# The causal mask of the diagonal score blocks: from a GpSimd multiply after the softmax numerator to an identity matmul into PSUM before it

## The chip, the cores and the metric

One core of one Trainium2 chip. The metric is the device time of one execution in microseconds. Engines are named as the profile names them: PE is TensorE (PEld its weight loads), DVE is VectorE, ACT is ScalarE, POOL is GpSimd, SP is SyncE, which only issues DMAs here.

## The reference

Two residual blocks over x of shape (2, 2048, 512) in float32. The first is causal attention with 16 heads of 32 features over a conditional linear layer, the second an adapter, a layer norm and an int8 linear layer. The change touches the attention:

```python
scores = jnp.einsum('bhtd,bhsd->bhts', q, k) * scale
alibi = -jnp.abs(rel).astype(jnp.float32) * alibi_slopes[None, :, None, None]
scores = scores + alibi
scores = jnp.where(causal[None, None], NEG, scores)      # causal = key after query
num = 0.5 * (1.0 + scores * jax.lax.rsqrt(1.0 + scores * scores))
probs = num / (jnp.sum(num, axis=-1, keepdims=True) + eps)
out = jnp.einsum('bhts,bhsd->bhtd', probs, v)
```

The softmax is a rational one: no maximum, no exponential. A masked score of -10000 has a numerator of about zero.

## The kernel before

The work is cut into 8 groups: 2 batches times 4 groups of 4 heads (`HG`). Within a group the 2048 queries are 4 chunks of 512 (c = 0 to 3), and chunk c meets the key blocks kb = 0 to 4c+3 of 128 keys each. One chunk and one key block are a unit (40 in a group); a unit has two pairs of heads, k = 2u and 2u+1, so a group has 80 pairs and the kernel 640. In scores keys lie on the partitions and queries along the free axis, two heads side by side.

The last four key blocks of every chunk lie on the diagonal (`g.diag`, 16 units and 32 pairs of a group, 256 pairs in all). There the queries before the key block are left out, so the widths of a pair are 1024, 768, 512 and 256 elements, two pairs of each in a chunk, and of what is left the first 128 queries of each head form the triangle that has to be masked. I call the 8 pairs on the diagonal of one chunk a diagonal stretch, and the pairs ahead of them, all 1024 wide, a full stretch (0, 8, 16 and 24 pairs for c = 0 to 3). There are 32 diagonal stretches.

For each pair, in this order:

1. PE writes two score matmuls into one of two PSUM slots `sc` (L835). It waits until DVE has read the pair two before (`s_g`).
2. ACT squares the scores into `yb` (L677), then takes 1/sqrt(1 + square) in place (L679). The `yb` ring has 4 places, so L677 waits for the numerator of the pair four before (`s_num`).
3. DVE forms g = score * y into `gb` (L1049). This frees the PSUM slot.
4. POOL squares y in place (L626); ACT takes (1 + g) squared in place, two pairs late (L669).
5. DVE adds the two, two pairs late (`NUM_LAG`, L990): y*y + (1+g)*(1+g) = 2(1+g), the numerator.
6. On diagonal pairs POOL multiplies the triangle's 128 queries of both heads by a 0/1 matrix `causal` (L605), after its own square of the pair two later (`MASK_LAG`).
7. PE multiplies the numerators of a whole unit with the values into `ov` and with ones into `dn` (L815), three units late (`LAG`). It waits for `s_mask` on diagonal units and for `s_num` on the others. At a chunk's first unit it waits for DVE to have copied the previous chunk out of `ov` and `dn` (L1003 and L1004, in the form for the previous group L1085 and L1086).

The order on every engine is written out by hand in `Group.events`; between the pairs lie parts of other jobs (projections of the next chunks at L731 and L735, the conditional layer at L748, and in some groups the adapter and the layer norm). Every engine works strictly along its list. The two middle head groups of each batch, 4 of the 8 groups, carry only the projections; I call them plain groups. The first group of batch 0 also makes the rest of that batch's conditional layer (opening), the last of batch 0 that of batch 1 (closing), the first of batch 1 the adapter work of batch 0 (joined), and the last one that of batch 1 (ending).

Of the kernel before, what the change touches and what calls it, by code (L numbers as in the profile page):

```python
# [7 lines left out]
ALU = mybir.AluOpType  # L8
# [8 lines left out]
P = 128  # L17
# [11 lines left out]
MASK_LAG = 2  # L29
# [3 lines left out]
MAGIC = 12582912.0  # L33
SOFT_EPS = 4e-6
# [129 lines left out]
def adaln_attn_ffn(nc, x, ids_cond, ids_lang, cond_w, cond_b, w_qkv, w_out, slopes, W1, b1, W2, b2,  # L164
# [34 lines left out]
    UNITS, PAIRS, DIAG = len(plain.units), 2 * len(plain.units), len(plain.diag)  # L199
# [39 lines left out]
    with ExitStack() as ctx:  # L239
# [21 lines left out]
        causal = sb("causal", [P, P])  # L261
# [53 lines left out]
        s_mask = sem("s_mask")  # L315
# [268 lines left out]
        def _(pool):  # L584
# [7 lines left out]
            pool.memset(causal[:, :], 1.0).then_inc(s_const, 1)  # L592
            pool.wait_ge(s_const, 6)
            pool.affine_select(out=causal[:, :], in_=causal[:, :], compare_op=ALU.is_ge, fill=0.0, base=0,
                               pattern=[[1, P]], channel_multiplier=-1).then_inc(s_const, 1)
            pool.memset(qmv[0:32, :, :, :].bitcast(F32), 0.0).then_inc(s_zero, 1)
            pool.wait_ge(s_al, 32)
            pool.memset(kst[0:32, :, :].bitcast(F32), 0.0).then_inc(s_zero, 1)

            def mask(G, g, k):  # L600

                q0 = q0_of(g, k)
                pool.wait_ge(s_num, G * PAIRS + k + 1)
                t = gview(k)[:, :, q0:q0 + P]
                pool.tensor_tensor(t, t, causal[:, :].unsqueeze(1).to_broadcast([P, 2, P]), ALU.mult).then_inc(s_mask, 1)  # L605
# [16 lines left out]
            def group(b, hg, G, g, base):  # L622
                def scored(k):
                    y = yview(k)[:, :, q0_of(g, k):]
                    pool.wait_ge(s_g, G * PAIRS + k + 1)
                    pool.tensor_tensor(y, y, y, ALU.mult).then_inc(s_y2, 1)  # L626
                    m = k - MASK_LAG
                    if (m >= 0 or g is not opening) and m // 2 % UNITS in g.diag:
                        mask(G, g, m)


                k = None
                for e in g.events:
                    if e[0] in ("qk", "pv") and k is not None:
                        scored(k)
                        k = None
                    if e[0] == "qk":
                        k = e[1]
                    elif e[0] == "step":
                        after(b if g is ending else b - 1, e[1], base)  # L640

            for_groups(pool, group)
            for m in range(-MASK_LAG, 0):
                mask(B * NG, plain, m)
# [59 lines left out]
        def _(pe):  # L704
# [98 lines left out]
            def products(G, g, u):  # L803

                c, kb = g.units[u % UNITS]
                q0 = g.width(u % UNITS)
                if u % UNITS in g.diag:
                    pe.wait_ge(s_mask, 2 * (G * DIAG + g.diag.index(u % UNITS) + 1 - (DIAG if u < 0 else 0)))
                else:
                    pe.wait_ge(s_num, G * PAIRS + 2 * u + 2)  # L810
                last_kb = kb == TT * (c + 1) - 1
                for dst, is_v in ((ov, True), (dn, False)):
                    for h in range(HG):
                        lhsT = vv[:, kb, h * D:(h + 1) * D] if is_v else ones[:, :]
                        r = pe.matmul(dst[h * D:(h + 1) * D, q0:], lhsT, gview(2 * u + h // 2)[:, h % 2, q0:],  # L815
                                      start=(kb == 0), stop=last_kb)
                r.then_inc(s_pv, 1)

            def group(b, hg, G, g, base):
                item, carry = 0, g is not opening  # L820
                for e in g.events:
                    if e[0] == "qk":
# [10 lines left out]
                        for i in range(2):  # L833
                            h = 2 * (k % 2) + i
                            r = pe.matmul(slot[:, i, q0:], kst[:, h, kb * P:(kb + 1) * P],  # L835
                                          qmv[:, c % 2, h, q0:], start=True, stop=True)
# [23 lines left out]

            for_groups(pe, group)
# [286 lines left out]
```

## Time and profile before

| | |
|---|---|
| median of 3 runs | 2297.26 us (2292.51 to 2299.26) |
| profiled execution, span from first to last instruction | 2294.5 us |
| PE busy | 1763.6 us (77%) |
| DVE busy | 1917.8 us (84%) |
| ACT busy | 1686.5 us (74%) |
| POOL busy | 1901.6 us (83%) |
| POOL mask multiplies (L605) | 256 instructions, 248.2 us |
| granted TensorE clock, mean | 0.903 |

Busy is the time in which the engine has an instruction running. No time is recorded for what surrounds the span of the profiled execution; the span is 2.8 us under the median of the runs. A granted clock of 1.00 is TensorE's full 2.4 GHz; it has one lower level, 1.2 GHz, and a figure between 0.5 and 1 is a mixture over the stretch. The pairs run from about 89 us to 2165 us of the span; what lies before is the preparation of the weights, what lies behind the end of the layer norm work and the int8 matmul.

### The profile page before, as it was taken

How to read it: one execution, taken by the hardware profiler on the slowest of the kernel's cores; microseconds unless marked ns; L12 is line 12 of the kernel's file. 1: busy time of each engine (PE TensorE's matmuls, PEld its weight loads, DVE VectorE, ACT ScalarE, POOL GpSimd, SP SyncE). 2: the span in 40 equal slices, each digit the busy share in tenths (PEclk: the TensorE clock that was granted, in tenths of full speed). 3: DMA queues.
4: the chain of work that ended last, by engine and by line, in shares of the span. 5: the costliest groups of instructions: out<-in, count | busy, mean ns of one | idle time of the engine just before them, and what ended most of it. 6: DMA issues, size and time to landing. Idle time of an engine off the chain costs nothing.

```text
span 2294.5 us, 30517 instructions
## 1 busy us (share of the span) xinstructions
PE 1763.6 (77%) x10128; PEld 873.0 (38%) x10128; DVE 1917.8 (84%) x2114; ACT 1686.5 (74%) x1938; POOL 1901.6 (83%) x1038
## 2 busy tenths in 40 slices
PE   5678877777787788998888876777687777786864
PEld 4555332323332345664444333333332333342331
DVE  4358888888889899898898898888889898899758
ACT  0247897889789888888656567889889888767413
POOL 2147998999989998898888888999989998898648
PEclk9899988888888899999999998888889898898879
DMA  5411111111111022202222221111111031121137
GB/s 177 140 48 43 48 34 30 47 40 30 34 39 48 20 80 60 69 18 81 76 75 80 65 57 30 43 44 27 38 39 48 20 85 39 39 65 47 51 123 239
DMA packets 126618, 138.64 MB, mean 60 GB/s; under 512 B 27868, under 2 KB 78044, under 8 KB 126044
## 3 DMA queue, kind: packets, MB, share of 16 engines
q1 hardware_dynamic: 126460, 136.64, 21.1%
q8 instruction: 86, 1.41, 0.3%
q14 instruction: 72, 0.59, 0.1%
HBM read 54.02 MB, written 22.80 MB: 33 GB/s over the span
## 4 chain that ended last, share of the span: by engine, by line
PE 24%; POOL 24%; DVE 19%; issue 14%; ACT 13%; SPq 2%; DMA 2%; DVEq 0%; POOLq 0%; ACTq 0%
POOL yb L626 18%; DVE gb L990 6%; ACT yb L677 6%; DVE gb L1049 5%; ACT yb L679 5%; PE sc L835 4%; PE ov L815 4%; PE it L748 3%; PE dn L815 3%; ACT gb L669 3%; PE it L731 3%; PE it L755 3%; POOL gb L605 2%; PE it L735 2%; POOL oT L662 2%
## 5 line engine op out<-in xcount | busy, mean ns | idle before, releaser
L626 POOL TENSOR_TENSOR yb<-yb 128x1024 f32<-128x1024 f32 (+3 forms) x640 | 1468.5, 2301 | 310.2 <-DVE gb L1049 296.0
L677 ACT ACTIVATE yb<-sc 128x1024 f32<-128x1024 f32 (+3 forms) x640 | 567.1, 886 | 398.8 <-PE sc L835 310.6
L990 DVE TENSOR_TENSOR gb<-gb,yb 128x1024 f32<-128x1024 f32 (+3 forms) x640 | 817.2, 1277 | 36.7 <-POOL yb L626 35.3
L1049 DVE TENSOR_TENSOR gb<-sc,yb 128x1024 f32<-128x1024 f32 (+3 forms) x640 | 676.4, 1057 | 150.3 <-ACT yb L679 147.2
L835 PE MATMUL sc<-qmv,kst 128*128 128x512 f32 (+3 forms) x1280 | 473.7, 458 | 333.7 <-DVE gb L1049 317.4
L679 ACT ACTIVATE yb<-yb 128x1024 f32<-128x1024 f32 (+3 forms) x640 | 595.1, 930 | 20.3
L669 ACT ACTIVATE gb<-gb 128x1024 f32<-128x1024 f32 (+3 forms) x640 | 584.1, 913 | 0.8 <-DVE gb L1049 0.8
L835 PEld LDWEIGHTS sc<-qmv,kst 128*128 128x128 f32 x1280 | 216.3, 206 | 699.8 <-DVE gb L1049 520.0
L815 PE MATMUL ov<-gb,vv 128*32 128x512 f32 (+3 forms) x2560 | 337.8, 603 | 37.2 <-DVE den L1086 15.3
L815 PE MATMUL dn<-gb,ones 128*32 128x512 f32 (+3 forms) x2560 | 326.4, 584 | 0.0
L731 PE MATMUL it<-hT,wT 128*128 128x512 f32 x496 | 254.6, 639 | 5.8 <-DVE area L928 1.8
L605 POOL TENSOR_TENSOR gb<-gb,causal 128x256 f32<-128x256 f32 x256 | 248.2, 970 | 0.0
L815 PEld LDWEIGHTS dn<-gb,ones 128*32 128x32 f32 x2560 | 89.4, 120 | 181.7 <-issue 176.2
L748 PE MATMUL it<-area 128*128 128x128 f32 x1024 | 131.3, 284 | 23.2 <-DVE area L911 21.8
L748 PEld LDWEIGHTS it<-area 128*128 128x128 f32 x1024 | 127.2, 199 | 31.7 <-DVE area L911 26.7
L731 PEld LDWEIGHTS it<-hT,wT 128*128 128x128 f32 x496 | 100.8, 205 | 87.2 <-issue 68.3
L735 PE MATMUL it<-wT,hT 128*128 128x128 f32 x992 | 128.0, 284 | 4.2 <-DVE stage L908 3.5
L735 PEld LDWEIGHTS it<-wT,hT 128*128 128x128 f32 x992 | 126.9, 200 | 11.4 <-DVE stage L908 3.8
L755 PE MATMUL it<-area,oT 128*128 128x512 f32 x224 | 116.2, 647 | 19.3 <-DVE area L918 6.4
L815 PEld LDWEIGHTS ov<-gb,vv 128*32 128x32 f32 x2560 | 52.8, 113 | 168.2 <-issue 115.8
L715 PE MATMUL it<-ident,area 128*128 128x128 f32 x336 | 53.0, 291 | 33.5 <-DMA area<-in_x_dram 13.0
L1014 DVE TENSOR_TENSOR oT<-oT,den 128x512 f32 (+1 forms) x31 | 65.9, 2124 | 1.9 <-DMA den<-rec_d 1.9
(109 smaller groups left out, 1020.4 us busy)
## 6 DMA issues: line engine op xcount, KB each, us to landing
qmv<-stage SPq DMA_DIRECT2D x384, 64.0 KB
kst<-stage SPq DMA_DIRECT2D x384, 64.0 KB
area<-in_x_dram SPq DMA_DIRECT2D x58, 256.0 KB, 2.8
out_dram<-oT SPq DMA_DIRECT2D x32, 256.0 KB, 3.5
den<-rec_d SPq DMA_DIRECT2D x31, 256.0 KB
wT<-wT_d SPq DMA_DIRECT2D x7, 768.0 KB, 4.4
x_d<-area SPq DMA_DIRECT2D x16, 256.0 KB, 2.6
z_d<-area SPq DMA_DIRECT2D x16, 256.0 KB, 3.1
```

What stands on the lines that cost most here:

```text
L605: pool.tensor_tensor(t, t, causal[:, :].unsqueeze(1).to_broadcast([P, 2, P]), ALU.mult).then_inc(s_mask, 1)
L626: pool.tensor_tensor(y, y, y, ALU.mult).then_inc(s_y2, 1)
L669: act.activation(t, t, ACT.Square, bias=1.0).then_inc(s_g2, 1)
L677: act.activation(y, sc[:, k % SLOTS, :, q0_of(g, k):], ACT.Square).then_inc(s_s2, 1)
L679: act.activation(y, y, ACT.Abs_reciprocal_sqrt, bias=1.0).then_inc(s_y, 1)
L731: r = pe.matmul(bank, wT[:, "qk".index(what), part, :], hT[:, part, c * CH:(c + 1) * CH], **ends)
L735: r = pe.matmul(bank[:, part * P:(part + 1) * P], hT[:, k, tok], wT[:, 2, k, :], start=(k == 0), stop=(k == KC - 1))
L748: r = pe.matmul(bank[:, part * P:(part + 1) * P], wc[:, k, part * P:(part + 1) * P], xT[:, a, k, :], start=(k == 0), stop=(k == KC - 1))
L815: r = pe.matmul(dst[h * D:(h + 1) * D, q0:], lhsT, gview(2 * u + h // 2)[:, h % 2, q0:], start=(kb == 0), stop=last_kb)
L835: r = pe.matmul(slot[:, i, q0:], kst[:, h, kb * P:(kb + 1) * P], qmv[:, c % 2, h, q0:], start=True, stop=True)
L990: dve.tensor_tensor(t, t, yview(k)[:, :, q0:], ALU.add).then_inc(s_num, 1)
L1049: dve.tensor_tensor(gview(k)[:, :, q0:], sc[:, k % SLOTS, :, q0:], yview(k)[:, :, q0:], ALU.mult).then_inc(s_g, 1)
```

## The change

The mask is no longer multiplied onto the weights. A constant 128x128 matrix `unseen`, -1e12 where the key lies after the query and 0 elsewhere, is made once, as is a bf16 copy of it and of the identity. Behind each score matmul of a diagonal pair PE issues one more matmul, identity times `unseen16`, 128 columns in bf16, which accumulates onto the first 128 queries of that head's scores in PSUM. At -1e12 the two squares that follow add to nearly zero. POOL's `mask` and its semaphore are gone, and the products wait for `s_num` in every unit.

```diff
-MASK_LAG = 2
+UNSEEN = -1e12
...
-            pool.memset(causal[:, :], 1.0).then_inc(s_const, 1)
+            pool.memset(unseen[:, :], 0.0).then_inc(s_const, 1)
             pool.wait_ge(s_const, 6)
-            pool.affine_select(out=causal[:, :], in_=causal[:, :], compare_op=ALU.is_ge, fill=0.0, base=0,
+            pool.affine_select(out=unseen[:, :], in_=unseen[:, :], compare_op=ALU.is_ge, fill=UNSEEN, base=0,
                                pattern=[[1, P]], channel_multiplier=-1).then_inc(s_const, 1)
+            pool.wait_ge(s_const, 7)
+            pool.tensor_copy(unseen16[:, :], unseen[:, :]).then_inc(s_const, 1)
+            pool.tensor_copy(ident16[:, :], ident[:, :]).then_inc(s_const, 1)
...
-            def mask(G, g, k):
-
-                q0 = q0_of(g, k)
-                pool.wait_ge(s_num, G * PAIRS + k + 1)
-                t = gview(k)[:, :, q0:q0 + P]
-                pool.tensor_tensor(t, t, causal[:, :].unsqueeze(1).to_broadcast([P, 2, P]), ALU.mult).then_inc(s_mask, 1)
...
                     pool.tensor_tensor(y, y, y, ALU.mult).then_inc(s_y2, 1)
-                    m = k - MASK_LAG
-                    if (m >= 0 or g is not opening) and m // 2 % UNITS in g.diag:
-                        mask(G, g, m)
...
-                if u % UNITS in g.diag:
-                    pe.wait_ge(s_mask, 2 * (G * DIAG + g.diag.index(u % UNITS) + 1 - (DIAG if u < 0 else 0)))
-                else:
-                    pe.wait_ge(s_num, G * PAIRS + 2 * u + 2)
+                pe.wait_ge(s_num, G * PAIRS + 2 * u + 2)
...
+                            on_diagonal = k // 2 in g.diag
                             r = pe.matmul(slot[:, i, q0:], kst[:, h, kb * P:(kb + 1) * P],
-                                          qmv[:, c % 2, h, q0:], start=True, stop=True)
+                                          qmv[:, c % 2, h, q0:], start=True, stop=not on_diagonal)
+                            if on_diagonal:
+                                r = pe.matmul(slot[:, i, q0:q0 + P], ident16[:, :], unseen16[:, :], start=False, stop=True)
...
+            pe.wait_ge(s_const, 9)
             for_groups(pe, group)
```

What stands on PE in the last two units of a chunk's diagonal, before (ov and dn are the products with the values and with ones, sc the scores):

```order
L835 MATMUL sc<-qmv,kst 128x256 [waits s_g]
L835 MATMUL sc<-qmv,kst 128x256
L815 MATMUL ov<-gb,vv 32x512 [waits s_num]
L815 MATMUL ov<-gb,vv 32x512 x3
L815 MATMUL dn<-gb,ones 32x512 x4
```

and after the change, at the same place, for the pair ahead of the same products:

```order
L825 MATMUL sc<-qmv,kst 128x256 [waits s_g]
L828 MATMUL sc<-unseen,ident 128x128
L825 MATMUL sc<-qmv,kst 128x256
L828 MATMUL sc<-unseen,ident 128x128
L804 MATMUL ov<-gb,vv 32x512 [waits s_num]
```

Each pair has two more matmuls, each with a weight load of its own, between and behind the score matmuls; nothing else on PE has changed its place. On POOL a diagonal stretch reads, before:

```order
L626 TENSOR_TENSOR yb<-yb 128x2x384 [waits s_g]
L605 TENSOR_TENSOR gb<-gb,causal 128x2x128 [waits s_num]
L625 REGISTER_ALU
L626 TENSOR_TENSOR yb<-yb 128x2x256 [waits s_g]
L605 TENSOR_TENSOR gb<-gb,causal 128x2x128 [waits s_num]
```

and after:

```order
L623 TENSOR_TENSOR yb<-yb 128x2x384 [waits s_g]
L622 REGISTER_ALU
L623 TENSOR_TENSOR yb<-yb 128x2x256 [waits s_g]
L622 REGISTER_ALU
L623 TENSOR_TENSOR yb<-yb 128x2x256 [waits s_g]
```

POOL's list is the squares alone, and it no longer waits for anything that DVE does after g. The lists of ACT, DVE and SP are the same as before.

## Rows read from the trace of the kernel before

**Rows 1.** The page, part 1: busy, share of the span, instructions

```profile
PE 1763.6 (77%) x10128; PEld 873.0 (38%) x10128; DVE 1917.8 (84%) x2114; ACT 1686.5 (74%) x1938; POOL 1901.6 (83%) x1038
```

**Rows 2.** Busy by stretch: diagonal stretches of the plain groups, sum of 16

```profile
core 0: us, PE busy (x) PEld busy (x) DVE busy (x) ACT busy (x) POOL busy (x), PEclk, DMA share, GB/s
...
493.79:514.92 21.13, 14.93 (x92) 4.91 (x82) 17.62 (x17) 17.15 (x25) 20.84 (x14) 0.84 0.00 1
...
sum 345.12, PE 253.41 PEld 94.21 DVE 279.60 ACT 273.04 POOL 329.86; mean PE 15.84 PEld 5.89 DVE 17.47 ACT 17.06 POOL 20.62
```

**Rows 3.** Busy by stretch: full stretches of the plain groups, sum of 12

```profile
sum 595.12, PE 456.48 PEld 207.11 DVE 533.99 ACT 549.02 POOL 529.96; mean PE 38.04 PEld 17.26 DVE 44.50 ACT 45.75 POOL 44.16
```

**Rows 4.** Busy by stretch: diagonal stretches of the other groups, sum of 16

```profile
94.13:143.37 49.24, 33.67 (x209) 26.66 (x210) 20.73 (x28) 15.87 (x23) 18.24 (x14) 0.90 0.19 49
...
893.24:915.12 21.88, 20.22 (x166) 13.61 (x164) 19.51 (x23) 17.13 (x26) 21.88 (x15) 1.00 0.21 57
...
1257.27:1290.15 32.88, 27.80 (x136) 12.33 (x134) 29.06 (x47) 15.44 (x23) 30.55 (x22) 0.90 0.20 55
...
sum 400.31, PE 314.38 PEld 162.03 DVE 327.65 ACT 263.57 POOL 347.14; mean PE 19.65 PEld 10.13 DVE 20.48 ACT 16.47 POOL 21.70
```

**Rows 5.** Timeline, 500 to 517: start, us, instruction, idle before it

```profile
508.95 1.94 PE L815 MATMUL ov<-gb,vv 128*32 128x512 f32 x8
...
509.25 0.38 ACT L677 ACTIVATE yb<-sc 128x256 f32<-128x256 f32 x1 [1.56 <-DVE gb L990]
...
510.00 0.73 POOL L605 TENSOR_TENSOR gb<-gb,causal 128x256 f32<-128x256 f32 x1
510.08 1.20 DVE L990 TENSOR_TENSOR gb<-gb,yb 128x512 f32<-128x512 f32 x1 [0.60 <-POOL yb L626]
...
512.77 1.02 ACT L677 ACTIVATE yb<-sc 128x1024 f32<-128x1024 f32 x1 [2.17 <-PE sc L835]
...
516.23 2.00 POOL L626 TENSOR_TENSOR yb<-yb 128x1024 f32<-128x1024 f32 x1 [0.38 <-DVE gb L1049]
```

**Rows 6.** Groups by line and shape: xcount, busy us, mean ns, idle before

```profile
L605 POOL TENSOR_TENSOR gb<-gb,causal 128x256 f32<-128x256 f32 x256 | 248.2, 970 | 0.0
...
L990 DVE TENSOR_TENSOR gb<-gb,yb 128x512 f32<-128x512 f32 x64 | 67.6, 1056 | 23.9 <-POOL yb L626 23.9
...
L1049 DVE TENSOR_TENSOR gb<-sc,yb 128x512 f32<-128x512 f32 x64 | 43.3, 676 | 1.6 <-ACT yb L679 1.6
```

**Rows 7.** Timeline, a full stretch: nine squares in a row; a numerator

```profile
541.01 26.40 POOL L626 TENSOR_TENSOR yb<-yb 128x1024 f32<-128x1024 f32 x9 [1.67 <-DVE gb L1049]
...
543.79 1.22 DVE L990 TENSOR_TENSOR gb<-gb,yb 128x1024 f32<-128x1024 f32 x1
```

**Rows 8.** Timeline and groups: runs of 128-column matmuls on PE

```profile
99.36 6.41 PE L748 MATMUL it<-area 128*128 128x128 f32 x56
```

**Rows 9.** One line, L880 and L748: ns min/median/max, bf16 and f32

```profile
L880 PEld LDWEIGHTS sc<-wT,yb x128: 95/98/147, 2232.0 to 2281.8; 128*128 128x128 bf16 x128
...
L748 PEld LDWEIGHTS it<-area x1024: 186/192/338, 18.1 to 1033.5; 128*128 128x128 f32 x171
L748 PE MATMUL it<-area x1024: 270/275/553, 18.2 to 1033.6; 128*128 128x128 f32 x171
```

**Rows 10.** Waits: who for whom, us in total, times, longest

```profile
ACT yb L677 <- PE sc L835: 310.6, 166, 19.0
...
PEld ov L815 <- POOL gb L605: 21.5, 23, 3.5
...
PE ov L815 <- POOL gb L605: 10.7, 13, 2.6
```

**Rows 11.** Timeline, 384 to 401, the turn from chunk 0 to chunk 1

```profile
391.00 1.94 PE L815 MATMUL ov<-gb,vv 128*32 128x512 f32 x8 [2.78 <-DVE den L1086]
...
394.57 1.55 PE L835 MATMUL sc<-qmv,kst 128*128 128x512 f32 x4
...
395.69 1.02 ACT L677 ACTIVATE yb<-sc 128x1024 f32<-128x1024 f32 x1 [4.56 <-PE sc L835]
```

More of the change, by code:

```diff
@@ L198, in adaln_attn_ffn @@
                         after_jobs(j, first[j // TT + 1] + 2 * LAG + 2 * NORM_LAG + 3, first[NC] - 9 + j - KB + TT, first[NC] - 1)], False, slack=0.3)
-    UNITS, PAIRS, DIAG = len(plain.units), 2 * len(plain.units), len(plain.diag)
+    UNITS, PAIRS = len(plain.units), 2 * len(plain.units)
     assert PAIRS % YRING == 0 and PAIRS % GRING == 0
@@ L260, in adaln_attn_ffn @@
         ones = sb("ones", [P, D])
-        causal = sb("causal", [P, P])
+        unseen = sb("unseen", [P, P])
+        unseen16 = sb("unseen16", [P, P], BF16)
+        ident16 = sb("ident16", [P, P], BF16)
         cbias = sb("cbias", [P, KC])
@@ L314, in adaln_attn_ffn @@
         s_num = sem("s_num")
-        s_mask = sem("s_mask")
         s_pv = sem("s_pv")
@@ L642, in _ @@
             for_groups(pool, group)
-            for m in range(-MASK_LAG, 0):
-                mask(B * NG, plain, m)
             for job in END_JOBS:
```

## The prediction

> **What bounds the kernel now.** I read the page first. Four engines are busy for 74 to 84% of the span [rows 1], so no engine bounds the whole kernel, and the share of POOL that the mask takes (248 us [rows 6]) says nothing yet. The question is which engine is full in the stretches where the mask is. So I cut the span where DVE starts the g of the first pair of each full and each diagonal stretch, and read the busy time of every engine in each piece.
>
> In the plain groups the 12 full stretches (192 pairs) last 595.1 us, 3.10 us a pair; ACT is busy for 549.0 of it, 92%, DVE and POOL for 534 and 530 [rows 3]. In the 16 diagonal stretches (128 pairs) it is otherwise: 345.1 us, 21.6 a stretch, of which POOL is busy for 329.9, 96%, DVE for 279.6, ACT for 273.0 and PE for 253.4 [rows 2]. There POOL is the bound, and by a wide margin: 20.6 us a stretch against 17.5, 17.1 and 15.8. In the other groups' 16 diagonal stretches POOL is first too, with 347.1 of 400.3 us, but DVE has 327.7 and PE 314.4 [rows 4].
>
> The timeline shows how POOL's lateness reaches the rest: DVE's numerator stands idle for 0.60 us until POOL's square is there, and ACT's next square waits 1.56 us for a numerator, because the ring `yb` is full [rows 5]. The mask also reaches DVE directly. The numerator that starts at 510.08 beside a mask takes 1.20 us; over all its 64 instances that shape takes 1.056 us, while g, of the same width but with one input in PSUM, takes 0.676 [rows 5, 6].
>
> **The change, part by part.**
>
> *The mask leaves POOL.* 256 instructions of 0.970 us, 248 us of POOL time [rows 6]. In a plain diagonal stretch that is up to 8 x 0.970 = 7.8 us (6 of its own in most windows, as two masks run into the next stretch), so POOL falls from 20.6 us to some 13 to 15. DVE gets back what the overlap cost: 1.056 - 0.676 = 0.38 us on a numerator at 512 wide is the most that it can be; at 0.3 us for 8 numerators it falls from 17.5 to about 15. ACT's 17.1 us does not move. With PE as it is, ACT would be next, at 17.1.
>
> *Two matmuls a pair are added to PE.* No row of before has this bf16 matmul. A run of 56 f32 matmuls of 128 columns, each with its weight load, takes 6.41 us, 0.114 us for load and matmul together at the full clock [rows 8]. A bf16 weight load takes 98 ns where the f32 one takes 192 [rows 9], so 0.114 is a ceiling for throughput at the full clock. The floor is nothing, if the two fit where PE idles. I take 0.114: 16 matmuls in a stretch are 1.8 us at full clock. The quoted stretch has a granted clock of 0.84 [rows 2], and if the added work fell wholly on the 1.2 GHz level it would be 3.7 us. PE then has 15.8 + 1.8 = 17.6 us, up to 19.5 us, and is the fullest engine, ahead of ACT. [...]
>
> *What a plain diagonal stretch then takes.* POOL at 20.6 us busy gave 21.6 us, 96%. PE is interrupted more often, since it takes turns with ACT and DVE through two PSUM slots; with PE at 17.6 us and 94% I get 18.8 us. That is 2.8 us less than 21.6, times 16: **-45 us**. Bounds: ACT's busy time alone, 17.1 us a stretch, gives -72; PE at 19.5 us and 93% gives 21.0 and -10.
>
> *The other groups' diagonal stretches.* The first, 49.2 us, has POOL busy for only 18.2 [rows 4], so it gains nothing. In the other fifteen, 351 us, POOL has 328.9 us and DVE 306.9. DVE has more other work here, as in the stretch of 32.9 us with DVE at 29.1 and POOL at 30.6, and in the closing group PE has 20.2 of 21.9 us at full clock [rows 4]; 1.8 us more there fills the stretch by itself. What DVE can get back is 15 x 8 x 0.3 = 36 us, the most that this part can gain is thus about 45, and the least about 5. I take 1.7 us a stretch: **-26 us**.
>
> *The masks that run over.* After each of 24 diagonal stretches that is followed by a full one, two masks run at the start of the full stretch, against 1024 wide squares and numerators. ACT bounds those stretches, so most is hidden; I take 0.4 us each: **-10 us**, between 0 and -20.
>
> *The added time lies on the way from score to ACT.* At the turn of a chunk ACT waits for PE already: 2.17 us at 512.77, behind 1.94 us of products at half clock [rows 5], and 4.56 us at 395.69, where PE first waited 2.78 us for DVE to empty `dn`, then needed 3.6 us for products (391.00 to 394.57) before the next score [rows 11]. Three more matmul pairs pass ahead of such a score in the same time. I take 0.5 us for each of the 24 turns: **+12 us**, between 0 and 25. Within a stretch PE has the score of a pair ready ahead of ACT, except in the 256 wide pairs, and I add nothing.
>
> *The wait of the products.* On diagonal units PE waited for the mask 10.7 us (13 times) and its weight loads 21.5 us [rows 10]. The products of unit u stand behind the scores of pair 2u+7, which wait for g of pair 2u+5; on DVE the numerator of pair 2u+1 precedes that g. So `s_num` is always there in time, and this wait ends. It is inside the terms above. Nothing new is queued behind it. The two POOL copies at the start and PE's wait for `s_const` cost nothing: the pairs begin near 89 us and the constants are made at the head of POOL's list, ahead of a long idle time.
>
> Sum: -45 - 26 - 10 + 12 = -69 us against the profiled execution's 2294.5 us: 2225.5. The median of the runs is 2.8 us above that span, so I predict **2228 us**.
>
> **The shared port, as a check.** Nine squares of 1024 take 26.40 us, 2.93 each, beside DVE's numerator of 1.22 [rows 7]; one with DVE idle takes 2.00 [rows 5]. So POOL and DVE cost each other about 0.8 us a pair. The Trainium skill (SBUF — State Buffer, Who interferes with whom) says that a VectorE instruction with two SBUF inputs and a GpSimd instruction take turns on one port, the later one blocked entirely. By that rule a pair of a full stretch would need 2.00 + 1.22 = 3.22 us on the port; the trace has 2.93, so they overlap in part. The rule would put the mask's price at its own 0.73 us plus the same again on DVE, and the gain nearer to that of the second case below.
>
> **The rivals.**
>
> *Larger gain, 2165 us, chance 0.18.* PE's matmuls fit into its idle time and bring a higher granted clock (0.84 in the quoted stretch), and DVE gets everything back. Then ACT is the bound: -72 - 45 - 15 = -132 from 2297. For it: PE is idle for a quarter of these stretches. Against it: at the turns ACT already waits for PE with POOL's lateness not in the chain.
>
> *Nearly nothing, 2282 us, chance 0.12 (half of it within 0.3% of before).* POOL's lateness only hid that of DVE and PE: -10 - 5 and +12 at the turns, and a few us of run-over masks, give -8 to -20. For it: DVE has 17.5 and 29.1 us in stretches of 21 and 33. This is also the case in which the change removes work and no wait.
>
> *Slower, 2360 us, chance 0.08.* The two matmuls lie in the ring PE, ACT, DVE, PE over two PSUM slots. A single 128-column matmul takes 0.275 us from start to end [rows 9], and if each of the two adds that whole, a pair is 0.55 us later, 256 x 0.55 = +141 us. Against that stand the -81 us of the first three terms: +60, 2357 or about 2360. It decides from 81/256 = 0.32 us a pair on the path. Against it: such matmuls follow each other every 0.114 us, and PE idles before most scores.
>
> **How the numbers follow.** My forecast has 0.62, with 2195 to 2262 as its own range. Faster by over 0.3% (about what a measurement of this kernel can tell from none): 0.62 + 0.18 + 0.06 = 0.86; within 0.3%: 0.06; slower: 0.08. The range reaches from inside the larger gain to inside the small one, 2175 to 2275, which leaves out under 2 in 10.
>
> **What would show it.** POOL's busy time down by some 248 us, to 1650; the 512 wide numerator down from 1.056 to near 0.7 us; the diagonal stretches of the plain groups at 18 to 19.5 us with PE the fullest engine, full stretches within 1 us of before; each added matmul spaced by 0.06 to 0.12 us. I am wrong if those stretches stay above 20.5 us, or if PE's wait for g shrinks while ACT's wait for scores (310.6 us now [rows 10]) grows by more than it.

## The result and the profile after

The changed kernel takes 2266.89 us (median of 4 runs, 2263.74 to 2269.1) against 2297.82 us for the kernel before on the same chip. The ratio is 0.9875, with a 95% interval of 0.9863 to 0.9888. That is a gain of 31 us by the medians, 26 to 31 us by the interval. It is faster, as forecast, and inside the range of 2175 to 2275, but the forecast gain was 69 us: less than half of it came. The profiled execution's span is 2263.8 us, against 2294.5.

The page of the kernel after, parts 1 and 4 (busy time of each engine; then the chain that ended last, by engine):

```profile
PE 1803.9 (80%) x10640; PEld 904.5 (40%) x10640; DVE 1878.6 (83%) x2114; ACT 1685.0 (74%) x1938; POOL 1715.7 (76%) x784
...
PE 38%; ACT 21%; DVE 20%; issue 12%; POOL 4%; DMA 2%; SPq 2%; DVEq 0%; POOLq 0%; ACTq 0%
```

POOL lost 186 us of busy time [rows 1], where 248 us of masks were taken away, and POOL has all but left the chain, where it had 24% before; PE went from 24% to 38%. The squares (L626, now L623) had 18% of the chain before; they have 16 us of it now, under 1%, and most of the 4% left is outside the attention. Of the missing 62 us, 42 went into longer squares (busy for 1468.5 us before and 1510.2 now), and 18 were never there to be freed, since the records of the masks overlapped those of POOL's other work. The groups by line and shape, beside [rows 6] (columns as there):

```profile
L623 POOL TENSOR_TENSOR yb<-yb 128x1024 f32<-128x1024 f32 x448 | 1189.2, 2663 | 394.1 <-DVE gb L1042 382.2
...
L983 DVE TENSOR_TENSOR gb<-gb,yb 128x1024 f32<-128x1024 f32 x448 | 613.3, 1369 | 1.7
...
L623 POOL TENSOR_TENSOR yb<-yb 128x768 f32<-128x768 f32 x64 | 155.8, 2448 | 38.0 <-DVE gb L1042 37.9
L828 PE MATMUL sc<-unseen,ident 128*128 128x128 bf16 x512 | 121.8, 243 | 0.0
L623 POOL TENSOR_TENSOR yb<-yb 128x512 f32<-128x512 f32 x64 | 108.9, 1713 | 15.1 <-DVE gb L1042 15.1
...
L983 DVE TENSOR_TENSOR gb<-gb,yb 128x512 f32<-128x512 f32 x64 | 56.0, 875 | 1.5 <-ACT gb L661 0.5 <-POOL yb L623 0.3
...
L828 PEld LDWEIGHTS sc<-unseen,ident 128*128 128x128 bf16 x512 | 52.6, 103 | 47.8 <-issue 27.6
```

The squares got longer. At 512 wide they took 1537 ns before and take 1713 now, at 768 wide 2247 and now 2448. That they run beside DVE's numerators more of the time is my reading; run 12 below shows that the squares slow the numerators. DVE's numerator at 512 wide fell from 1056 to 875 ns only, not to the 700 that I had named; over all 640 numerators the mean went from 1277 to 1218 ns, 38 us, where I had counted on up to 77.

The diagonal stretches of the plain groups, cut as in [rows 2]:

```profile
374.05:396.86 22.81, 16.81 (x114) 7.57 (x113) 15.72 (x21) 16.09 (x25) 14.50 (x8) 0.78 0.15 37
...
490.06:510.84 20.78, 16.07 (x104) 6.25 (x96) 16.78 (x17) 17.37 (x25) 16.36 (x9) 0.84 0.01 2
...
sum 339.12, PE 273.12 PEld 113.92 DVE 265.05 ACT 269.94 POOL 261.63; mean PE 17.07 PEld 7.12 DVE 16.57 ACT 16.87 POOL 16.35
```

PE's 17.1 us and ACT's 16.9 are what the forecast said (17.6 and 17.1), and POOL is down to 16.4. But the stretch takes 21.2 us, not 18.8: no engine is busy for more than 81% of it, where POOL had 96% of the time before. The full stretches of the plain groups, cut as in [rows 3]:

```profile
sum 589.52, PE 459.71 PEld 207.30 DVE 526.02 ACT 551.39 POOL 504.24; mean PE 38.31 PEld 17.27 DVE 43.84 ACT 45.95 POOL 42.02
```

All 640 pairs, cut in the same way (us; the sum of each kind, and what lies behind the last g):

| | before | after | difference | forecast |
|---|---|---|---|---|
| plain groups, 16 diagonal stretches | 345.1 | 339.1 | -6.0 | -45 |
| other groups, 16 diagonal stretches | 400.3 | 394.5 | -5.8 | -26 |
| all 24 full stretches | 1325.3 | 1312.4 | -12.9 | -10 |
| turns of a chunk (inside the rows above) | | | | +12 |
| behind the last g | 129.6 | 124.0 | -5.6 | 0 |

Every difference of stretches here and below comes from one profiled execution of each kernel. By chunk, the plain diagonal stretches changed by +0.8, -5.6, -1.1 and -0.2 us (c = 0 to 3, four stretches each): nearly all of the gain is in chunk 1. The plain full stretches changed by -5.1 us at chunk 1, +0.6 at chunk 2 and -1.1 at chunk 3.

The last row is a term that I left out. Behind the last g the last masks and the products that wait for them ended 7.2 us later in the kernel before and end 2.4 us later now, and the rest of the program follows them.

Why the diagonal stretches hardly moved is seen in what each engine waited for there. Idle time before an instruction, by what ended it, summed over the 16 plain diagonal stretches (us, waits of more than 0.15 us alone; "no mask" is run 1 below, without POOL's mask and without the matmuls):

| who waits, for what | before | no mask | after |
|---|---|---|---|
| DVE's numerator, for POOL's square | 19.6 | none | 0.3 |
| ACT's square, for a numerator (the ring `yb` is full) | 22.2 | 6.8 | 7.1 |
| ACT's square, for a score of PE | 43.8 | 48.0 | 57.8 |
| DVE's g, for ACT | 23.3 | 23.3 | 31.3 |
| PE's score, for g | 73.4 | 64.8 | 54.1 |

The two waits that POOL caused are gone or down to a third. But ACT was idle for 66.0 us in these stretches before and is for 64.9 now: it waits for scores instead of numerators. Twice as much of its idle time was for scores as for numerators even in the kernel before. The chain says the same. In the stretch that [rows 2] shows, POOL was busy for 20.84 of 21.13 us, and it has no piece of the chain there (before, 493.79 to 514.92, by line; the view cuts the line off):

```profile
by line: issue 24.0%; DVE gb L1049 13.9%; ACT yb L677 12.6%; ACT yb L679 11.8%; ACT gb L669 9.9%; PE ov L815 8.8%; PE sc L835 6.4%; PE dn L815 5.6%; DVE oT L1014 3.7%; DVE gb L990 2.9%; DVEq L1048 0.4%; DVEq L1011 0.2%; DVEq L1012 0.2%; DVE
```

Over the 16 plain diagonal stretches before, POOL has 62 of the chain's 345 us, in five of the stretches, and PE has 100. After, POOL has none and PE 155.

The chain from 493 to 508, in order of time (start, us, what), shows what stands in a diagonal stretch now:

```profile
493.01 1.24 DVE gb L1042
494.25 0.04 issue
494.29 0.69 PE sc L825
494.98 0.13 PE sc L828
495.11 0.43 PE sc L825
495.54 0.13 PE sc L828
495.67 1.87 PE ov L804 x8
497.53 1.71 PE dn L804 x8
499.24 0.51 PE sc L825
...
502.74 1.47 issue
504.21 0.09 DVE oT L1007
...
504.81 0.69 DVE gb L1042
...
505.54 0.33 PE sc L825
505.87 0.07 PE sc L828
505.94 0.12 PE sc L825
506.06 0.07 PE sc L828
506.13 1.00 PE ov L804 x8
507.13 0.86 PE dn L804 x8
```

Two kinds of work stand ahead of a score: 3.6 us of products at the 1.2 GHz level (granted clock 0.50 from 494.25 to 500.4; the same products take 1.9 us from 506.13, at 1.00), and on DVE a numerator and a division of the previous chunk (L1007) ahead of the g that frees the PSUM slot. Neither has a term of its own in my sum, except products at the turns. The experiments ask whether they are the reason.

### The profile page after: what moved, and what is told of

Read it like the earlier page. It is cut to its first block, busy times and chain, and to the rows that moved or that the text cites. A ratio compares the mean times of both kernels' runs of the same rounds, so it can differ in the third digit from the quotient of the medians.

```text
span 2263.8 us, 31228 instructions
## 1 busy us (share of the span) xinstructions
PE 1803.9 (80%) x10640; PEld 904.5 (40%) x10640; DVE 1878.6 (83%) x2114; ACT 1685.0 (74%) x1938; POOL 1715.7 (76%) x784
## 4 chain that ended last, share of the span: by engine, by line
PE 38%; ACT 21%; DVE 20%; issue 12%; POOL 4%; DMA 2%; SPq 2%; DVEq 0%; POOLq 0%; ACTq 0%
ACT yb L669 9%; PE sc L825 7%; PE ov L804 7%; ACT yb L671 7%; DVE gb L1042 6%; PE dn L804 6%; ACT gb L661 6%; DVE gb L983 5%; PE it L723 5%; PE it L740 4%; PE it L747 4%; PE it L727 3%; POOL oT L654 2%; SPq L428 2%; PE it L707 1%
## 5 line engine op out<-in xcount | busy, mean ns | idle before, releaser
L623 POOL TENSOR_TENSOR yb<-yb 128x1024 f32<-128x1024 f32 (+3 forms) x640 | 1510.2, 2373 | 460.9 <-DVE gb L1042 448.6
L983 DVE TENSOR_TENSOR gb<-gb,yb 128x1024 f32<-128x1024 f32 (+3 forms) x640 | 779.2, 1218 | 3.9 <-ACT gb L661 0.5
L825 PE MATMUL sc<-qmv,kst 128*128 128x512 f32 (+3 forms) x1280 | 505.6, 472 | 295.8 <-DVE gb L1042 278.2
L825 PEld LDWEIGHTS sc<-qmv,kst 128*128 128x128 f32 x1280 | 238.7, 209 | 648.3 <-DVE gb L1042 453.3
L804 PE MATMUL ov<-gb,vv 128*32 128x512 f32 (+3 forms) x2560 | 338.4, 604 | 18.0 <-DVE den L997 10.5
L723 PE MATMUL it<-hT,wT 128*128 128x512 f32 x496 | 249.9, 629 | 5.8 <-DVE area L921 1.8
L727 PEld LDWEIGHTS it<-wT,hT 128*128 128x128 f32 x992 | 121.1, 194 | 8.8 <-DVE stage L901 2.5
L828 PE MATMUL sc<-unseen,ident 128*128 128x128 bf16 x512 | 121.8, 243 | 0.0
L804 PEld LDWEIGHTS ov<-gb,vv 128*32 128x32 f32 x2560 | 52.4, 112 | 133.4 <-issue 82.2
L899 DVE TENSOR_SCALAR stage<-it 128x512 fp32r<-128x512 f32 x64 | 43.7, 683 | 34.7 <-PE it L723 20.8
```

The costliest lines, as they stand in the source:

```text
L723: r = pe.matmul(bank, wT[:, "qk".index(what), part, :], hT[:, part, c * CH:(c + 1) * CH], **ends)
L727: r = pe.matmul(bank[:, part * P:(part + 1) * P], hT[:, k, tok], wT[:, 2, k, :], start=(k == 0), stop=(k == KC - 1))
L983: dve.tensor_tensor(t, t, yview(k)[:, :, q0:], ALU.add).then_inc(s_num, 1)
```

## The experiments

Every ratio is to the kernel before, measured on the same chip in turns (its medians: 2296.09 us beside runs 1 to 4, 2292.79 beside 5 to 8, 2295.05 beside 9 to 11, 2296.70 beside 12 and 13). "Plain" is the sum of the plain groups' 16 diagonal stretches, "diagonal" that of all 32. The expectations of runs 1 to 4 are by two theories: A, that POOL's lateness lay beside other waits that are nearly as long, so that its mask is worth little and the matmuls cost little; B, that the POOL mask is worth the forecast 81 us and the matmuls take some 50 of them back.

**1 to 4. The two prices apart.** No mask at all (the output then lacks it):

```diff
                             r = pe.matmul(slot[:, i, q0:], kst[:, h, kb * P:(kb + 1) * P],
-                                          qmv[:, c % 2, h, q0:], start=True, stop=not on_diagonal)
-                            if on_diagonal:
-                                r = pe.matmul(slot[:, i, q0:q0 + P], ident16[:, :], unseen16[:, :], start=False, stop=True)
+                                          qmv[:, c % 2, h, q0:], start=True, stop=True)
```

> The changed kernel without the added matmuls: the causal mask is left out altogether, so keys after the query count in the diagonal blocks. Theory A (POOL's lateness lay beside a wait of PE, ACT and DVE on each other that is nearly as long, and the added matmuls cost little): 2255 to 2265 us, at most 12 us under the changed kernel's 2266.9. Theory B (taking the mask off POOL is worth the forecast 81 us, and the added matmuls take some 50 of them back): about 2220 us, under 2235 in any case.

Both masks, POOL's multiplies and PE's matmuls:

```diff
+                    if (m >= 0 or g is not opening) and m // 2 % UNITS in g.diag:
+                        mask(G, g, m)
...
+                if u % UNITS in g.diag:
+                    pe.wait_ge(s_mask, 2 * (G * DIAG + g.diag.index(u % UNITS) + 1 - (DIAG if u < 0 else 0)))
```

> The changed kernel with POOL's multiply put back as well, so both masks are applied: POOL is as loaded as before and PE as loaded as after. Theory A: 2296 to 2305 us, within 8 us of the kernel before, since PE's added time lies under POOL's lateness. Theory B: the added matmuls cost some 50 us here too, 2330 us or more, unless POOL's lateness hides them. Together with the run without any mask this gives the price of each of the two, with and without the other.

The mask matmul issued twice for each head:

```diff
+                                r = pe.matmul(slot[:, i, q0:q0 + P], ident16[:, :], unseen16[:, :], start=False, stop=False)
                                 r = pe.matmul(slot[:, i, q0:q0 + P], ident16[:, :], unseen16[:, :], start=False, stop=True)
```

> The changed kernel with every mask matmul issued twice (the constant is added two times). Theory A: 5 to 10 us over the changed kernel, 2272 to 2277. Theory B: as much again as the first matmuls took, 2300 us or more.

Both score matmuls of a pair first, then both mask matmuls:

```diff
-                            if on_diagonal:
-                                r = pe.matmul(slot[:, i, q0:q0 + P], ident16[:, :], unseen16[:, :], start=False, stop=True)
+                        if on_diagonal:
+                            for i in range(2):
+                                r = pe.matmul(slot[:, i, q0:q0 + P], ident16[:, :], unseen16[:, :], start=False, stop=True)
```

> The changed kernel with both score matmuls of a pair first and the two mask matmuls behind them, so that the second score matmul's weights load under the first one as before the change. In the trace of the changed kernel a pair's scores are complete about 0.20 us later than before at full clock. Theory A: 0 to 3 us faster than the changed kernel, 2264 to 2267. Theory B: a third or more of the price of the matmuls comes back, 2250 us or less.

| | POOL mask | mask matmuls | us | ratio (95%) | plain | diagonal |
|---|---|---|---|---|---|---|
| before | yes | 0 | 2296.09 | 1 | 345.1 | 745.4 |
| 2, both | yes | 2 a pair | 2310.59 | 1.0063 (1.0037 to 1.0089) | 353.3 | 751.8 |
| after | no | 2 a pair | 2266.89 | 0.9875 (0.9863 to 0.9888) | 339.1 | 733.6 |
| 3, twice | no | 4 a pair | 2275.37 | 0.9905 (0.9881 to 0.9929) | 345.6 | 742.5 |
| 4, masks last | no | 2 a pair | 2260.36 | 0.9841 (0.9818 to 0.9864) | 335.5 | 731.9 |
| 1, no mask | no | 0 | 2256.19 | 0.9817 (0.9788 to 0.9846) | 330.2 | 720.7 |

The matmuls cost 13.3 us without the POOL mask (0.9875 less 0.9817, of 2296) and 14.5 us with it; two more a pair cost 7 us. With the intervals these are 6 to 21, 8 to 20 and 1 to 13 us. Taking the mask off POOL is worth 42 us without the matmuls (40 by the medians) and 43 with them, so the two prices add up. Runs 1 and 3 lie in A's ranges, and B failed in all four. A failed in run 2, where it had at most 8 us over the kernel before: the matmuls cost as much in stretches in which POOL is busy for 94% of the time as in those where it is not, so a full POOL does not hide them. Run 4 is faster than A's range and slower than B's. The surprise is run 1: with no mask anywhere, the kernel gains only 40 us. My forecast has ACT as the bound in that case, at 17.1 us a stretch; it is 330.2 / 16 = 20.6, with ACT busy for 82% of it:

```profile
sum 330.21, PE 253.45 PEld 92.24 DVE 269.42 ACT 270.25 POOL 265.99; mean PE 15.84 PEld 5.77 DVE 16.84 ACT 16.89 POOL 16.62
```

Masks last is the best version that computes all of it: 7.8 us below the change as made by the ratios. It is not certain: the two intervals touch (0.9864 and 0.9863), and its profiled execution has a span of 2264.9 us, beside 2263.8.

**5 to 8. Products ahead of a score, and the division (theories P and D).** First the products were split, those with the values ahead of the odd pair's scores, those with ones behind them:

```diff
+                        if k % 2 and early(g, k // 2 - LAG):
+                            products(G, g, k // 2 - LAG, (0,))
...
-                        products(G, g, u)
+                        products(G, g, u, (1,) if early(g, u) else (0, 1))
```

> The changed kernel with the products of a unit in two parts: the four matmuls into ov are issued ahead of the odd pair's scores, the four into dn stay behind them (a chunk's first unit stays whole). Work, buffers and the DVE list are the same. Theory P (what took POOL's place is PE: a block of 2.0 us of products, 3.6 at half clock, stands between an odd and an even pair's scores, and ACT runs dry behind it): 8 to 20 us faster than the changed kernel, 2247 to 2259. Theory D (it is DVE's list: the division, the copies and the numerators that stand ahead of g): no change, 2264 to 2270.

Then chunk 1's division was moved to a later pair, into the full stretch:

```diff
-                lag = NORM_LAG_LAST if c == NC - 1 else NORM_LAG
+                lag = NORM_LAG_LAST if c == NC - 1 else 3 if c == 1 else NORM_LAG
```

> The changed kernel with the division of chunk 1 (one 2 us instruction of DVE in each of the 8 groups) moved from the narrow pairs of chunk 2's diagonal, at pair 45, to pair 38 of its full stretch. Theory D: g of pair 45 no longer stands behind it, 1 to 2 us a group, 8 to 16 us faster, 2251 to 2259. Theory P: 0 to 4 us faster, since PE's products are next at the same place.

Then the products with ones were left out, except at the first and the last key block of a chunk, in the kernel after and in the one before (the denominators are then too small):

```diff
-                for dst, is_v in ((ov, True), (dn, False)):
+                for dst, is_v in ((ov, True), (dn, False))[:2 if kb == 0 or last_kb else 1]:
```

> The changed kernel without most of the denominators' products: the four matmuls into dn are issued for the first and the last key block of a chunk alone, so the denominators are too small. PE loses some 250 us of its work and the block ahead of the next scores is halved. Theory P: the diagonal stretches of the plain groups fall to 18.5 us or less and the whole to 2220 us or less. Theory D: 2250 us or more.

> The kernel before with the same products left out. Theory P: POOL is the bound with or without PE's products, so it stays within 20 us of the kernel before, 2277 to 2297, and its distance to the changed kernel with the same omission is 60 us or more, near the 81 that was forecast for the relief of POOL. Theory D: the distance stays at 30 to 40 us.

| | us | ratio (95%) | plain | diagonal |
|---|---|---|---|---|
| 5, split | 2274.61 | 0.9917 (0.9895 to 0.9938) | 338.4 | 736.3 |
| 6, division moved | 2278.34 | 0.9931 (0.9913 to 0.9949) | 332.1 | 723.9 |
| 7, after, few products | 2238.66 | 0.9746 (0.9721 to 0.9771) | 332.5 | 719.8 |
| 8, before, few products | 2277.10 | 0.9925 (0.9905 to 0.9945) | 339.0 | 741.0 |

Both rearrangements are slower than the change as made (0.9875), by 10 and 13 us, and neither theory had that: P expected run 5 to be faster and D run 6, and none expected a slower kernel. The moved division did shorten the plain diagonal stretches by 7.0 us, but the plain full stretches grew from 589.5 to 601.0: it costs more there, where ACT is busy for 94% of the time. Run 7 is also between the theories: its plain diagonal stretches take 20.8 us each and not 18.5, but its time is under D's 2250. With half of the products gone the change is worth 38 us instead of 31, as D had it, not the 60 and more of theory P. Leaving the products out gives 30 us in the kernel after (0.9875 to 0.9746) and 17 in the one before: PE is nearer to the bound after the change, but these products account for 7 of the 38 us that lie between the 69 forecast and the 31 measured.

**9. The granted clock (theory K).** Ten bf16 matmuls of zeros were added behind the even diagonal pairs of chunks 1 to 3:

```diff
+                        if c and k % 2 == 0 and k // 2 in g.diag:
+                            for _ in range(10):
+                                pe.matmul(dn[:, 0:P], zero16[:, :], ident16[:, :], start=False, stop=False)
```

> The changed kernel with ten bf16 matmuls of a zero matrix, 128 columns each, accumulated onto dn behind the scores of every even diagonal pair of chunks 1 to 3: they add nothing to the result and keep TensorE at work where it idles 1.6 to 2.1 us for DVE's g. Theory K (the lower clock, 0.75 to 0.92 in these stretches of the plain groups, is what makes the products behind it long, 3.6 us where full clock takes 2.0): the granted clock of these stretches rises to 0.95 or more and the time falls by 10 to 20 us, to 2247 to 2257. Theory T (PE, ACT and DVE wait for each other in turn and each is nearly as long as POOL was): the clock may rise, but the ten matmuls stand ahead of the next scores and DVE is next anyway: 2262 to 2275.

2281.35 us, ratio 0.9949 (0.993 to 0.9967), 17 us slower than the change as made, and outside both theories' ranges. The granted clock of those twelve plain stretches went from between 0.84 and 1.00 to 1.00 in ten of them, and to 0.95 and 0.91 in the other two. All 16 plain stretches together take 339.4 us, where they took 339.1, but that hides three different things (us, four stretches each):

| | chunk 0, no zeros | chunk 1 | chunk 2 | chunk 3 |
|---|---|---|---|---|
| after | 93.0 | 77.6 | 84.7 | 83.9 |
| with zeros | 94.9 | 77.8 | 80.3 | 86.5 |

At chunk 2 the clock of all four rose from between 0.84 and 0.87 to 1.00, and each is 0.7 to 1.5 us shorter, as K would have it, 4.4 us in all; in the other chunks the sums did not fall. In the closing group, where PE is full, the full stretches grew by 4.3 us and the diagonal ones by 4.6. So the zeros cost more than the clock gave back.

**10 and 11. Products and division both relieved.** Few products with ones, and the division cut to one column (the output of the attention is then not divided):

```diff
-                dve.tensor_tensor(o, o, den[:, :], ALU.mult).then_inc(s_norm, 1)
+                dve.tensor_tensor(o[:, 0:1], o[:, 0:1], den[:, 0:1], ALU.mult).then_inc(s_norm, 1)
```

> The changed kernel without most of the denominators' products, as in the last pair of experiments, and with each 2 us division of DVE in the loop cut to one column, so that the output is not normalised: PE loses some 250 us of work and DVE some 60. Theory T: with PE and DVE both relieved nothing stands in POOL's place but ACT: 2205 us or less. Theory C (the mask off POOL is worth 40 us whatever the others do, since its time on the shared port returns as longer squares and numerators): 2225 us or more.

> The kernel before with the same two omissions. Theory T: POOL still bounds its diagonal stretches, 2260 to 2275 us, and the distance to the changed kernel with the same omissions is 55 us or more. Theory C: the distance stays at 35 to 45 us.

2234.28 us, ratio 0.9740 (0.9723 to 0.9758) for the kernel after, and 2252.71 us, 0.9822 (0.9801 to 0.9842) for the one before. Run 10 by itself is as C had it, but run 11 is below T's range, and the difference of the two is 18 us, under what either theory gave, so both failed. The finding is by ratios beside runs 7 and 8: the cut division gives 24 us while POOL has its masks, and 1 to 4 us without them. The plain diagonal stretches did not move (334.3 and 339.9). In the kernel before POOL is busy for 326.5 of the 339.9 us; after the change no engine is above 82%. All versions with the squares in them stay at 20.6 us a stretch or more.

**12 and 13. The squares and the mask.** One thing that all these versions share is POOL's squares beside DVE's numerators. Here the diagonal pairs' squares are taken on 16 queries of each head only (the rest of y*y is left out), in the kernel after and in the one before:

```diff
+                    if k // 2 in g.diag:
+                        y = y[:, :, 0:16]
                     pool.tensor_tensor(y, y, y, ALU.mult).then_inc(s_y2, 1)
```

> Leaves most of the diagonal pairs' y*y out: on POOL only the first 16 queries of each head are squared, so in a diagonal stretch POOL works some 2 us instead of 12, and takes no time from DVE. The mask is in the PE matmuls as in the kernel after. Theory S (what is left of the plain diagonal stretches, 21.2 us each, hangs on POOL and DVE sharing time: squares of up to 2.66 us and numerators of 1.37): the plain diagonal stretches fall from 339.1 to below 315 us in sum, all 32 from 733.6 to below 695, and the time from 2267 to 2225 to 2235. Theory R (it hangs on the ring PE, ACT, DVE over two PSUM slots, in which POOL's square has no part, and on ACT and DVE work that stays): the plain diagonal stretches stay above 330, and the time is 2255 to 2267.

> The kernel before with the same cut: POOL's squares on diagonal pairs on 16 queries of each head only, so POOL's share there is its mask multiplies (7.8 us a stretch) and little else. If POOL's total length is what the mask costs in the kernel before, the mask is now hidden, and moving it to PE is worth nothing or loses: this kernel is at most 3 us slower than the kernel after with the same cut, or up to 14 us faster (what the two matmuls a pair cost in the runs with and without them). If the mask's place in the order (numerator, then mask, then products) or its sharing of time with DVE costs by itself, this kernel is 10 us or more slower than it.

| | squares whole | squares cut | the cut is worth |
|---|---|---|---|
| mask on POOL: us (ratio) | 2297 (1) | 2235.29 (0.9727) | 61 us |
| mask on PE: us (ratio) | 2267 (0.9875) | 2246.01 (0.9780) | 21 us |
| moving the mask is worth | -31 us | +10.7 us | |
| diagonal, mask on POOL | 745.4 | 693.0 | 52.4 |
| diagonal, mask on PE | 733.6 | 715.1 | 18.5 |

The differences are those of the medians; by the ratios the cut is worth 63 and 22 us. The intervals are 0.9707 to 0.9747 and 0.9764 to 0.9797. Once POOL has room, the change of this document makes the kernel 10.7 us slower: 22.1 us more in the diagonal stretches, 9.5 less in the full ones (1322.2 to 1312.7), where the masks that run over no longer stand, and 1.6 less behind the last g. The plain groups' diagonal stretches, cut as in [rows 2], mask on PE first:

```profile
418.60:438.11 19.51, 17.24 (x124) 7.24 (x123) 15.73 (x20) 16.65 (x25) 8.52 (x9) 0.91 0.19 51
...
sum 332.01, PE 271.09 PEld 113.35 DVE 245.64 ACT 268.99 POOL 122.16; mean PE 16.94 PEld 7.08 DVE 15.35 ACT 16.81 POOL 7.63
```

and mask on POOL:

```profile
419.45:437.50 18.05, 14.53 (x110) 5.79 (x108) 16.16 (x20) 16.48 (x25) 13.50 (x15) 1.00 0.21 56
...
sum 313.28, PE 235.09 PEld 89.11 DVE 252.84 ACT 269.14 POOL 204.54; mean PE 14.69 PEld 5.57 DVE 15.80 ACT 16.82 POOL 12.78
```

With the mask on POOL they are 19.6 us each, the first of all versions under 20.5; with the mask on PE 20.8, where PE is busy for 16.9 us a stretch instead of 14.7. With the mask on PE, DVE's numerators fell from 1292 to 991 ns at 768 wide and from 875 to 708 at 512 as the squares beside them were cut; with the mask on POOL those at 512 fell from 1056 to 976. For run 12 neither theory was right: the stretches stayed above 330 us as R says, the time came out between the two, as did the sum over all 32. For run 13 the first branch was right: with POOL's time short enough, its mask is hidden.

## Why the prediction fell short

**"There POOL is the bound, and by a wide margin": half right.** POOL was the fullest engine, and its lateness cost time: leaving out its squares gives 61 us, 52 of them in the diagonal stretches. But it was not the bound alone and not by a wide margin. Leaving out its masks gives 40 us, the added matmuls lengthened the plain diagonal stretches by 8.2 us while POOL was full (345.1 to 353.3, run 2), and ACT was idle for scores twice as long as for anything that POOL held up. I read the margin from busy times, 20.6 against 17.5, and a busy time says nothing of how long the waits of the others are.

**"What a plain diagonal stretch then takes", 18.8 us: the step that failed.** I took the fullest engine's busy time, PE's 17.6, and divided it by 94%. The busy time was right (17.1), the 94% was not: it was 81%. A share of 96% was what one overfull engine reached. With four engines at 16.4 to 17.1 us, each of which takes turns with the others, the stretch has no such engine. The matmuls on PE are not the reason: without them (run 1) the share is 82% and the stretch 20.6 us. What the runs show in place of my step is that the waits changed hands. Without the POOL mask and with nothing added, ACT's idle time in these stretches fell by 11.2 us in sum (66.0 to 54.8), DVE's for squares by 19.6, and the stretches by 14.9, where my step would have given 54 (ACT's 17.1 us by 94% is 18.2 a stretch); with the matmuls ACT's idle time is back at 64.9. Which wait between PE, ACT and DVE holds the stretch at 20.6 us is not shown: relieving PE (run 7), PE and DVE (run 10) and the clock (run 9) each left the mean above 20.5, and only cutting POOL's squares with the mask on POOL (run 13) brought it lower.

**The turns, +12 us: wrong.** The turn that I quoted shows nothing: ACT waits 4.62 us for the score at 394.71, where it waited 4.56 before [rows 11]. Over all 24 turns ACT's idle time before the first pair's square fell, from 64.7 to 58.0 us, and it is 60.1 without the matmuls (run 1). The matmuls' price is real, 13 us, but it lies within the diagonal stretches (733.6 against 720.7), where I had counted the matmuls as busy time of PE and added nothing for them on the way from score to ACT.

**The other groups, -26 us: DVE's relief was mis-sized**, and the term measured -5.8. DVE's busy time there fell by 9.6 us (327.7 to 318.1), where I had up to 36, and PE's grew by 22.5 (314.4 to 336.9); one stretch of the opening group grew from 23.9 to 26.3 us. What DVE gets back was sized at 0.3 us for each numerator. It is 0.18 at 512 wide and 0.17 at 256 (592 to 427 ns), nothing at 768 (1263 to 1292), 0.04 at 1024. My reading is that the squares, which now stand closer to the numerators, took it; no run shows that by itself. The row behind my check by the shared port was misread a little: the square of 2.00 us at 516.23 had no numerator beside it for most of its time, but DVE was not idle, its g ran from 517.23. By that check each mask would have cost DVE another 0.73 us; DVE's busy time fell by 39 us for all 256, 0.15 each.

**The masks that run over: right in sum** (-12.9 against -10), by luck in its parts. I had 0.4 us at each of 24 stretches. The plain groups' full stretches of chunk 1 went from 26.0 to 26.3 down to 24.9 us each, and those of chunks 2 and 3 by 0.5 in sum over eight. **The drain behind the last g, -5.6 us, was left out.**

**The added matmul: right.** In the chain above it has 0.13 us at the 1.2 GHz level, and 0.07 at the full clock (505.87); I had said 0.06 to 0.12. A load takes 96 ns by the median where the f32 one takes 192; that is a factor of two, as in [rows 9]. The Trainium skill (TensorE: Matmul & The Clock Gate, Weight-path perf modes) says that the fast load reads two bf16 weights at a time and gives about two times as measured on this chip; the trace agrees.

**The signs that I named.** The stretches stayed above 20.5 us, so by my own bound I was wrong there; POOL's busy time is 1716 us and not 1650, and the 512 wide numerator 0.875 us and not 0.7. The other sign did not fire: ACT's wait for scores grew by 27 us, from 310.6 to 337.2, less than PE's wait for g shrank, from 317.4 to 278.2. The rows of after:

```profile
PE sc L825 <- DVE gb L1042: 278.2, 222, 8.4
...
ACT yb L669 <- PE sc L825: 189.8, 108, 14.4
...
ACT yb L669 <- PE sc L828: 147.4, 90, 19.3
```

**The rival "nearly nothing"** was nearer to the time (2282, against my 2228 and the measured 2267). Its reason, that POOL's lateness hid that of DVE and PE, is what the runs show in part. "Slower" put 0.55 us a pair on the path; it is 13 / 256 = 0.05, far under the 0.32 from which that rival decides. With POOL given room by the cut squares the sign is the rival's, +10.7 us.

**What stays open.** Even with short squares and no mask matmuls a plain diagonal stretch is 19.6 us with ACT busy for 16.8. A part is the turn from chunk 0 to chunk 1, where such a stretch took 22.1 us against 18.1 to 20.7 in the chunks behind it in the same group. I did not run a version without that turn, nor one without squares and without any mask. How squares and numerators slow each other was seen by their durations alone. Why run 10 gained so little from the shorter division, where run 11 gained 24 us, is open too.

## What to carry to other kernels

With one engine at 96% of a stretch and three others at 73 to 81%, taking its masks away, and with them 19% of its busy time, shortened the stretch by 4% (run 1), and by 2% with the work put on another engine, not by the gap to the next engine: the share that one overfull engine reaches is no share for four that take turns. Before the margin to the next engine is believed, add up what the other engines wait for in the same stretches; here most of ACT's idle time was for scores of PE and not for anything of POOL's. Before work is moved to another engine, try a run in which it is simply gone (run 1, 40 us); here it bounded the gain from above. If the engine that is to be relieved does two jobs, weigh both: here leaving out most of the other job's diagonal part was worth 61 us, and it turned the move of this one into a loss.

## What the runs showed of the hardware that I had not expected

- POOL's time isn't freed one for one: 248 us of masks gone, 186 us of busy time less. The squares took 9 to 14% longer at 768, 512 and 256 wide (2247 to 2448, 1537 to 1713, 813 to 926 ns), 42 us of busy time in all. The mask itself took 970 ns in the kernel before and 803 ns in run 13.
- A bf16 identity matmul of 128 columns behind an f32 score matmul has a record of 230 ns, and 0.07 us in the chain at the full clock: the rest overlaps its neighbours. All 512 cost the kernel 13.3 us (6 to 21 by the intervals), 0.026 each.
- Matmuls of zeros raised the granted clock in ten of the twelve stretches in which they stood, but only the four of chunk 2 got shorter for it (84.7 to 80.3 us in sum, at 1.00 instead of 0.84 to 0.87), and the kernel became 17 us slower.
- A numerator of DVE got shorter when POOL's squares beside it were cut: 1292 to 991 ns at 768 wide, 875 to 708 at 512 (run 12). So the work of one engine made the instructions of another longer, here by up to 30%.
